# Attention with score products in bursts of three pairs on a three-entry PSUM ring

## The chip, the cores and the metric

One NeuronCore of one Trainium2 chip runs the kernel. The metric is device time in microseconds for one launch. In the profile PE is TensorE (PEld its weight loads), DVE VectorE, ACT ScalarE, POOL GpSimd, SP the engine that issues most DMAs.

## The reference

Cross-attention with 16 heads of 16 and a residual, then a mixture of 8 experts of which each token takes 2. The change touches the attention alone; what is computed is not changed.

```python
q, k, v = split(layernorm(x) @ wq.T + bq), split(ctx @ wk.T + bk), split(ctx @ wv.T + bv)
attn = softmax(einsum('bhqd,bhkd->bhqk', q, k) / 4)            # B=8, H=16, 512 x 512
x = x + (einsum('bhqk,bhkd->bhqd', attn, v) joined) @ wo.T + bo
x = x + sum over the top 2 of 8 experts: gate * (gelu(layernorm(x) @ W1 + b1) @ W2 + b2)
```

## The kernel before

The program runs in two stages: attention for all 8 batches (to about 550 us), and behind it the experts on sorted tokens. It is written engine by engine, each with its own program, and semaphores between them.

Attention is cut into 32 *units* u (batch i, group g of four heads), each unit into 8 *slots* p: one tile of 128 keys and two heads. For each slot of each unit two products of the same operands are made on TensorE, each a *pair* of matmuls (64 rows of the array for either head, 512 columns), into one entry of a ring of three PSUM tiles of 128 x 1024:

- `score(v, p)` (L1224, matmul L1233 of the page; MX in what follows): scores with queries on the partitions. DVE takes their row maximum (`reduce_max`, TENSOR_REDUCE at L860) into `negm`. It runs two units ahead: with slot (u, p) stands the MX of (u + 2, p) (`ahead`, L139).
- `score_t(u, p)` (matmul L1246; ST): the same scores transposed, with the maximum already subtracted through an extra row. ACT takes their exponential (L784) into `probs`.

The names of the lines: in the profile the page gives L1233 for MATMUL ring<-k_st,q_st and L1246 for MATMUL ring<-q_st,k_st; the weights of the first are q_st, of the second k_st.

`ring_order` (L147) writes down the order in which entries of the ring are claimed; `ORDER` and `PLACE` make it a numbering, entry = number mod 3. `slot(n)` (L1214) lets PE wait until the reader of claim n - 3 is done: `exp_done` if it was an ST, `max_free` if it was an MX.

Beside its two pairs a slot has *other products*, all on PE:

- `pv` (L1259): four products of `probs` and the values into `ps_pv`, in the slots p = 0 (the last of the unit before), 2, 4 and 6. When a unit is complete ACT copies them out (`take_o`, L774).
- `misc` by the tables PREP, NEXT, POST and so on (L35 to L48): projections Q, K, V (L1287, L1297), transposes XT, CT, XG of inputs (L1277), MT (L1268, the transpose of the maxima, at p = 0), the output projection OP (L1305), logits LG and ranks PX. All share one bank, `ps_x`; `claim` lets PE wait until the reader of the one before is done. ACT copies out Q, K, V, XT, CT, XG and MT; DVE takes OP, LG and PX.

ACT's program (its `body`) is, for each slot in order: exponential of ST, at p = 0 the copy of the pv sums, then the copies of the slot's misc products. DVE's is: the maximum of the slot's MX, then the slot's OP, LG or PX, then pieces of layer norms and routing. Both wait for PE at each step, in this fixed order.

PE's program `body` (L1331) takes each slot by itself: ST, MX, then pv and misc of that slot. In the middle batches each slot has some other product. In unit 0 the first slots have one ST and two MX, and in unit 26 on some slots have no other product.

Of the kernel before, what the change touches and what calls it, by code (L numbers as in the profile page):

```python
# [21 lines left out]
G = NG * B  # L22
# [7 lines left out]
NP = NT * HPG // 2  # L30
# [76 lines left out]
def units(i, g, p):  # L107

    u, out = NG * i + g, []
    if p == (2 if u == 0 else 0) and u + 1 < G:  # L110
        out.append(("MT", u + 1))
    last = i == B - 1
    for table, b in (((LAST_LATE if last else LATE), i - 2), ((LAST_POST if last else POST), i - 1),
                     ((FIRST if i == 0 else PREP), i + 1), (NEXT, i + 2)):
        if 0 <= b < B and (g, p) in table:
            out.append((table[g, p], b))
    return out
# [21 lines left out]
def ahead(u, p):  # L139

    if u == 0:
        rest = [(1, q) for q in range(NP // 2, NP)] + [(2, q) for q in range(NP)]
        return rest[2 * p:2 * p + 2] if p < NP // 2 else rest[p + NP // 2:p + NP // 2 + 1]
    return [(u + 2, p)] if u + 2 < G else []


def ring_order():  # L147
    order = [("MX", v, p) for v, p in EARLY]
    for u in range(G):
        for p in range(NP):  # L150
            order += [("ST", u, p)] + [("MX", v, q) for v, q in ahead(u, p)]
    return order


ORDER = ring_order()
PLACE = {op: n for n, op in enumerate(ORDER)}


def build(nc, x, ctx_kv, wqT, bq, wkT, bk, wvT, bv, woT, bo, wg, bg, w1, b1, w2, b2, out):
    with ExitStack() as stack:  # L160
# [1042 lines left out]
        def _(pe):  # L1203
# [10 lines left out]
            def slot(n):  # L1214

                if n >= RINGS:
                    kind, u, p = ORDER[n - RINGS]
                    pe.wait_ge(exp_done if kind == "ST" else max_free, NP * u + p + 1)
                else:
                    for k in (2 * n, 2 * n + 1):  # L1220
                        pe.wait_ge(done[last[k][0]], last[k][1])
                return ring[n % RINGS]

            def score(v, p):  # L1224

                b, g = divmod(v, NG)
                kt, jp = divmod(p, 2)
                if p == 0:
                    pe.wait_ge(stack_in[g], 16 * (5 * b + 4))
                ps = slot(PLACE["MX", v, p])  # L1230
                for h in range(2):
                    lo = HALF * h
                    mm = nc.tensor.matmul(ps[:, h, :], q_st[lo:lo + HALF, 2 * g + jp, kt * P:(kt + 1) * P],  # L1233
                                          k_st[lo:lo + HALF, 2 * g + jp, :], start=True, stop=True)
                mm.then_inc(max_full, 1)

            def score_t(u, p):

                b, g = divmod(u, NG)
                kt, jp = divmod(p, 2)  # L1240
                if p == 0:
                    pe.wait_ge(m_in[g], 16 * (b + 1))
                ps = slot(PLACE["ST", u, p])
                for h in range(2):
                    lo = HALF * h
                    mm = nc.tensor.matmul(ps[:, h, :], k_st[lo:lo + HALF, 2 * g + jp, kt * P:(kt + 1) * P],  # L1246
                                          q_st[lo:lo + HALF, 2 * g + jp, :], start=True, stop=True)
                mm.then_inc(st_full, 1)

            def pv(u, kt):  # L1250

                b, g = divmod(u, NG)
                pe.wait_ge(exp_done, NP * u + 2 * (kt + 1))
                if kt == 0:
                    if u > 0:
                        pe.wait_ge(o_out, u)
                    pe.wait_ge(v_in, NG * b + g + 1)
                for j in range(HPG):
                    mm = nc.tensor.matmul(ps_pv[2 * DH * j:2 * DH * (j + 1), :], v_aug[:, kt, HPG * g + j, :],  # L1259
                                          probs[:, kt, j, :], start=(kt == 0), stop=(kt == NT - 1))  # L1260
                mm.then_inc(pv_done, 1)
# [69 lines left out]
            def body(i):  # L1331
                for g in range(NG):
                    u = NG * i + g
                    for p in range(NP):
                        score_t(u, p)
                        for v, q in ahead(u, p):
                            score(v, q)
                        if p == 0 and u > 0:
                            pv(u - 1, NT - 1)
                        if p in (2, 4, 6):  # L1340
                            pv(u, p // 2 - 1)
                        for name, b in units(i, g, p):
                            misc(name, b)
# [17 lines left out]
            for i in range(B):  # L1361
                body(i)
# [90 lines left out]
```

## Time and profile before

| | us |
|---|---|
| three timed runs | 869.04 (median), 860.61, 870.62 |
| the profiled execution | 858.64 |
| its span, first to last instruction | 856.8 |
| PE busy | 766.0 |
| DVE busy | 630.3 |
| ACT busy | 452.4 |

The difference of 858.64 and 856.8 lies around the span. A line of the page names the source line, the engine, the operation, the tile written and those read. "[x <-ENGINE ...]" behind a row is idle time of that engine before the instruction and who ended it; on the load queue (PEld) idle time is mostly the time in which PE works off the matmuls before.

### The profile page before, as it was taken

What the parts mean: (1) busy time and instruction counts of PE and PEld (TensorE: products, weight loads), DVE (VectorE), ACT (ScalarE), POOL (GpSimd) and SP (SyncE); (2) the same over time, 40 slices, a digit from 0 to 9 for tenths busy, and PEclk for the clock granted to TensorE, in tenths of its full rate; (3) what the DMA queues carried; (4) which work ended last, traced back from release to release, by engine and by line L of the source; (5) the groups of instructions that cost most, each with busy time, mean ns of one, the idle gap of its engine ahead of it and who ended that gap; (6) DMA issues with size and microseconds to landing.
All of it is one profiled execution on the core that took longest, in us unless ns stands there. A gap on an engine that the chain in (4) does not pass through costs nothing. (4 is left out here: it accounts for less than half of the span.)

```text
span 856.8 us, 16256 instructions
## 1 busy us (share of the span) xinstructions
PE 766.0 (89%) x4697; PEld 460.4 (54%) x4697; DVE 630.3 (74%) x1113; ACT 452.4 (53%) x669; POOL 370.7 (43%) x342
## 2 busy tenths in 40 slices
PE   8599899999999999999999787331999999999995
PEld 4243344444444444444444332120899999999995
DVE  6786777797797797897787875365677777777774
ACT  3066775766766767766666555220444444444442
POOL 6406153266276176176244052304244444444444
PEclk9589999999999999999999988655999999999998
DMA  6857575676675676567367332244244444444441
GB/s 216 206 152 212 134 202 180 172 227 198 173 244 167 175 244 181 149 229 202 109 219 213 90 110 69 89 196 134 46 80 77 79 81 74 78 75 78 77 75 13
DMA packets 89083, 122.60 MB, mean 143 GB/s; under 512 B 15032, under 2 KB 51864, under 8 KB 88744
## 3 DMA queue, kind: packets, MB, share of 16 engines
q1 hardware_dynamic: 74632, 103.69, 42.2%
q0 software_dynamic: 13296, 17.09, 11.2%
q8 instruction: 43, 0.70, 0.4%
q10 hardware_dynamic: 1072, 0.79, 0.3%
q14 instruction: 40, 0.33, 0.1%
HBM read 64.44 MB, written 57.22 MB: 142 GB/s over the span
## 5 line engine op out<-in xcount | busy, mean ns | idle before, releaser
L860 DVE TENSOR_REDUCE negm<-ring 128x2 f32<-128x1024 f32 x256 | 310.3, 1222 | 76.9 <-PE ring L1233 74.7
L784 ACT ACTIVATE probs<-ring 128x1024 f32<-128x1024 f32 x256 | 260.7, 1024 | 98.0 <-PE ring L1246 97.6
L706 POOL DMA_INDIRECT out<-y_sb,xs x71 | 110.6, 1557 | 150.5 <-DMA out<-y_sb,xs 81.9
L1259 PE MATMUL ps_pv<-probs,v_aug 128*32 128x512 f32 x1024 | 138.6, 613 | 5.3 <-ACT probs L784 5.2
L1246 PE MATMUL ring<-q_st,k_st 64*128 64x512 f32 x512 | 128.0, 499 | 4.6 <-DVE negm L860 4.5
L1233 PE MATMUL ring<-k_st,q_st 64*128 64x512 f32 x512 | 110.4, 432 | 12.7 <-ACT probs L784 5.7
L1246 PEld LDWEIGHTS ring<-q_st,k_st 64*128 64x128 f32 x512 | 48.3, 186 | 105.8 <-issue 76.4
L612 POOL DMA_INDIRECT xs_dram<-xg,rows x64 | 65.4, 1021 | 81.0 <-DVEq L1023 51.1
L1404 PE MATMUL ring<-w_hi,hT_hi 128*128 x284 | 85.7, 302 | 0.1
L1404 PE MATMUL ring<-w_lo,hT_hi 128*128 x284 | 80.4, 283 | 0.0
L1404 PE MATMUL ring<-w_hi,hT_lo 128*128 x284 | 79.7, 281 | 0.0
L1171 DVE TENSOR_TENSOR h_pre<-ring,b_sb 128x512 f32<-128x512 f32 x71 | 49.1, 691 | 35.8 <-PE ring L1386 35.7
L654 POOL TENSOR_TENSOR v_aug<-v_flat,bv_sb 128x256 f32<-128x256 f32 x32 | 23.0, 736 | 99.5 <-PE ps_pv L1259 89.2
L1233 PEld LDWEIGHTS ring<-k_st,q_st 64*128 64x128 f32 x512 | 50.9, 195 | 27.5 <-DVE negm L860 8.8
L827 ACT CAST xsT_hi<-ps_pv 128x256 fp32r<-128x256 f32 x36 | 13.4, 373 | 88.6 <-PE ps_pv L1377 88.6
L1386 PE MATMUL ring<-w_hi,xsT_hi 128*128 x142 | 56.8, 400 | 1.7 <-DVE xsT_lo L1159 1.7
L1386 PE MATMUL ring<-w_lo,xsT_hi 128*128 x142 | 56.7, 399 | 0.0
L638 POOL CAST qk_hi<-qk 128x512 fp32r<-128x512 f32 x28 | 17.1, 610 | 91.4 <-ACT qk L749 60.9
L1386 PE MATMUL ring<-w_hi,xsT_lo 128*128 x142 | 56.5, 398 | 0.0
L1305 PE MATMUL ps_x<-wo_sb,numT 128*128 128x256 f32 x128 | 40.8, 447 | 15.5 <-DVE numT L896 13.9
L1404 PEld LDWEIGHTS ring<-w_lo,hT_hi 128*128 128x128 f32 x284 | 53.9, 190 | 0.0
L1404 PEld LDWEIGHTS ring<-w_hi,hT_hi 128*128 128x128 f32 x284 | 53.8, 189 | 0.2 <-issue 0.2
(167 smaller groups left out, 1240.5 us busy)
## 6 DMA issues: line engine op xcount, KB each, us to landing
k_st<-k_dram SPq DMA_DIRECT2D x64, 192.0 KB
q_st<-q_dram SPq DMA_DIRECT2D x64, 192.0 KB
xs<-xs_dram SPq DMA_DIRECT2D x71, 132.5 KB, 2.3
k_dram<-qk_hi SPq DMA_DIRECT2D x32, 256.0 KB
q_dram<-qk_hi SPq DMA_DIRECT2D x32, 256.0 KB, 2.9
o_dram<-oT SPq DMA_DIRECT2D x32, 256.0 KB, 3.9
x_all<-in_x SPq DMA_DIRECT2D x8, 512.0 KB, 4.9
k_dram<-qk_lo SPq DMA_DIRECT2D x16, 256.0 KB
```

The source lines that it names most:

```text
L612: pool.indirect_dma_start(out=xs_dram, out_offset=bass.IndirectOffsetOnAxis(ap=rows[:, k, t:t + 1], axis=0), in_=xg[:, t, :], in_offset=No ...
L654: nc.gpsimd.tensor_tensor(v_aug[:, :, HPG * g:HPG * (g + 1), 0:DH], v_flat[:, :, heads].rearrange("p t (h d) -> p t h d", d=DH), bv_sb[:, ...
L706: pool.indirect_dma_start(out=out, out_offset=bass.IndirectOffsetOnAxis(ap=xs[:, j % AHEAD, TOKEN:TOKEN + 1].bitcast(I32), axis=0), in_=y_ ...
L784: nc.scalar.activation(probs[:, kt, 2 * jp:2 * jp + 2, :], ring[PLACE["ST", u, p] % RINGS][:], ACT.Exp).then_inc(exp_done, 1)
L860: nc.vector.tensor_reduce(negm[:, v % 2, :, jp, kt], ring[PLACE["MX", v, p] % RINGS][:], AX.X, ALU.max, negate=True).then_inc(max_free, 1)
L1171: v.tensor_tensor(h_pre[:, j % 2, :], ps_h[j % 2], b1_sb[:, bass.ds(e, 1), :].rearrange("p o h -> p (o h)"), ALU.add).then_inc(f_h_out, 1)
L1233: mm = nc.tensor.matmul(ps[:, h, :], q_st[lo:lo + HALF, 2 * g + jp, kt * P:(kt + 1) * P], k_st[lo:lo + HALF, 2 * g + jp, :], start=True, s ...
L1246: mm = nc.tensor.matmul(ps[:, h, :], k_st[lo:lo + HALF, 2 * g + jp, kt * P:(kt + 1) * P], q_st[lo:lo + HALF, 2 * g + jp, :], start=True, s ...
L1259: mm = nc.tensor.matmul(ps_pv[2 * DH * j:2 * DH * (j + 1), :], v_aug[:, kt, HPG * g + j, :], probs[:, kt, j, :], start=(kt == 0), stop=(kt ...
L1305: mm = nc.tensor.matmul(ps[:, (t % 2) * D:(t % 2 + 1) * D], numT[:, c, t * P:(t + 1) * P], wo_sb[:, c, :], start=(c == 0), stop=(c == DC - 1))
L1386: mm = nc.tensor.matmul(ps_h[j % 2], x[:, j % 2, c, :], w[:, bass.ds(e, 1), c, :].rearrange("p o h -> p (o h)"), start=(n == 0), stop=(n = ...
L1404: mm = nc.tensor.matmul(ps_y[j % 2][:, 0:D], h[:, j % 2, c, :], w[:, bass.ds(e, 1), c, :].rearrange("p o d -> p (o d)"), start=(n == 0), s ...
```

## The change

The slots are taken in threes from (1, 0) on, 231 slots in 77 triples; `third(u, p)` gives a slot's place in its triple (0, 1, 2) or None outside. The first slot issues its ST and MX and the ST of the second slot, then its other products. The second issues its own MX and the ST and MX of the third, then its other products. The third issues its other products alone. `ring_order` is written to match. ACT's and DVE's programs are not touched.

```diff
+def third(u, p):
+    n = NP * (u - 1) + p
+    return n % 3 if 0 <= n < NP * (G - 3) // 3 * 3 else None
+
+def after(u, p):
+    return (u, p + 1) if p + 1 < NP else (u + 1, 0)
+
 def ring_order():
     order = [("MX", v, p) for v, p in EARLY]
     for u in range(G):
         for p in range(NP):
-            order += [("ST", u, p)] + [("MX", v, q) for v, q in ahead(u, p)]
+            place, own, maxima = third(u, p), [("ST", u, p)], [("MX", v, q) for v, q in ahead(u, p)]
+            if place == 0:
+                order += own + maxima + [("ST", *after(u, p))]
+            elif place == 1:
+                order += maxima + [("ST", *after(u, p))] + [("MX", v, q) for v, q in ahead(*after(u, p))]
+            elif place is None:
+                order += own + maxima
     return order
...
                     for p in range(NP):
-                        score_t(u, p)
-                        for v, q in ahead(u, p):
-                            score(v, q)
+                        place = third(u, p)
+                        if place in (0, None):
+                            score_t(u, p)
+                        if place != 2:
+                            for v, q in ahead(u, p):
+                                score(v, q)
+                        if place in (0, 1):
+                            score_t(*after(u, p))
+                        if place == 1:
+                            for v, q in ahead(*after(u, p)):
+                                score(v, q)
                         if p == 0 and u > 0:
                             pv(u - 1, NT - 1)
```

PE in unit 20, slots (20, 3) to (20, 5), before; L1246 is ST, L1233 MX, L1287 a projection, L1259 pv:

```order
L1246 MATMUL ring0<-q_st,k_st 128x512 x2
L1233 MATMUL ring1<-k_st,q_st 128x512 x2
L1287 MATMUL ps_x<-xnT,wq_sb 128x256 x2
L1246 MATMUL ring2<-q_st,k_st 128x512 x2
L1233 MATMUL ring0<-k_st,q_st 128x512 x2
L1259 MATMUL ps_pv<-probs,v_aug 32x512 x4
L1246 MATMUL ring1<-q_st,k_st 128x512 x2
L1233 MATMUL ring2<-k_st,q_st 128x512 x2
L1287 MATMUL ps_x<-xnT,wq_sb 128x256 x2
```

The same place after, from the triple's first slot (20, 4) to its end; lines have moved by 16, so L1262 is ST, L1249 MX, L1303 a projection, L1275 pv:

```order
L1262 MATMUL ring2<-q_st,k_st 128x512 x2
L1249 MATMUL ring0<-k_st,q_st 128x512 x2
L1262 MATMUL ring1<-q_st,k_st 128x512 x2
L1275 MATMUL ps_pv<-probs,v_aug 32x512 x4
L1249 MATMUL ring2<-k_st,q_st 128x512 x2
L1262 MATMUL ring0<-q_st,k_st 128x512 x2
L1249 MATMUL ring1<-k_st,q_st 128x512 x2
L1303 MATMUL ps_x<-xnT,wq_sb 128x256 x2
L1275 MATMUL ps_pv<-probs,v_aug 32x512 x4
```

A pair and one ring entry stood beside each other product before; now three pairs stand together, all three entries of the ring, then one slot's other products, three pairs, and two slots' others. Each entry keeps its reader and its place in the claims. The second burst's last pair writes ring1, which the first burst's last pair filled, with one product between the bursts.

ACT in the same unit, the same before and after up to the line numbers (L784 the exponential, L746 the copy of a Q projection; before):

```order
L784 ACTIVATE probs<-ring0 128x1024
L746 ACTIVATE qk32<-ps_x,bq_sb 128x256
L784 ACTIVATE probs<-ring2 128x1024
L784 ACTIVATE probs<-ring1 128x1024
L746 ACTIVATE qk32<-ps_x,bq_sb 128x256
L784 ACTIVATE probs<-ring0 128x1024
```

A slot's copy stands between that slot's exponential and the next slot's, as it did.

## Rows read from the trace of the kernel before

**Rows 1.** The page: busy us, share and instructions; PE's busy tenths in 40 slices.

```profile
PE 766.0 (89%) x4697; PEld 460.4 (54%) x4697; DVE 630.3 (74%) x1113; ACT 452.4 (53%) x669; POOL 370.7 (43%) x342
PE   8599899999999999999999787331999999999995
```

**Rows 2.** Stretches: length, busy PE, PEld, DVE, ACT, POOL; PE clock, DMA share, GB/s.

```profile
62.00:440.00 378.00, 372.20 (x2254) 167.34 (x2246) 301.18 (x477) 258.28 (x345) 180.13 (x181) 1.00 0.65 189
...
460.00:470.00 10.00, 8.86 (x59) 3.60 (x59) 7.90 (x7) 7.46 (x11) 3.16 (x5) 1.00 0.80 193
...
480.00:490.00 10.00, 7.92 (x61) 2.86 (x63) 9.37 (x27) 5.81 (x7) 0.00 (x0) 1.00 0.55 118
490.00:500.00 10.00, 7.12 (x27) 2.96 (x26) 5.12 (x7) 3.16 (x5) 6.87 (x7) 0.66 0.48 163
```

**Rows 3.** Groups of instructions, 62 to 440 us: busy us, mean ns, idle before.

```profile
L860 DVE TENSOR_REDUCE negm<-ring 128x2 f32<-128x1024 f32 x198 | 241.1, 1223 | 60.9 <-PE ring L1233 59.2
L784 ACT ACTIVATE probs<-ring 128x1024 f32<-128x1024 f32 x198 | 202.2, 1024 | 62.7 <-PE ring L1246 62.7
```

**Rows 4.** PE in order of time, unit 20: start us, duration us, what.

```profile
355.19 1.06 PE L1259 MATMUL ps_pv<-probs,v_aug 128*32 128x512 f32 x8
356.19 1.13 PE L1287 MATMUL ps_x<-kvT,wk_sb 128*128 128x256 f32 x4
357.25 0.50 PE L1246 MATMUL ring<-q_st,k_st 64*128 64x512 f32 x2
...
358.97 0.50 PE L1246 MATMUL ring<-q_st,k_st 64*128 64x512 f32 x2
...
359.63 1.06 PE L1259 MATMUL ps_pv<-probs,v_aug 128*32 128x512 f32 x8
360.63 0.49 PE L1246 MATMUL ring<-q_st,k_st 64*128 64x512 f32 x2
...
361.29 1.13 PE L1287 MATMUL ps_x<-xnT,wq_sb 128*128 128x256 f32 x4
362.35 0.50 PE L1246 MATMUL ring<-q_st,k_st 64*128 64x512 f32 x2
```

**Rows 5.** ACT in order of time, unit 20.

```profile
361.16 1.02 ACT L784 ACTIVATE probs<-ring 128x1024 f32<-128x1024 f32 x1 [0.63 <-PE ring L1246]
362.46 0.47 ACT L746 ACTIVATE qk<-ps_x,bq_sb 128x256 f32<-128x256 f32 x1 [0.27 <-PE ps_x L1287]
362.89 1.03 ACT L784 ACTIVATE probs<-ring 128x1024 f32<-128x1024 f32 x1
```

**Rows 6.** PE in order of time, unit 0: one ST and two MX.

```profile
50.61 0.50 PE L1246 MATMUL ring<-q_st,k_st 64*128 64x512 f32 x2
...
51.50 1.13 PE L1287 MATMUL ps_x<-kvT,wk_sb 128*128 128x256 f32 x4
```

**Rows 7.** Engines in order of time, end of unit 26: a slot without other products.

```profile
458.76 0.19 PEld L1246 LDWEIGHTS ring<-q_st,k_st 64*128 64x128 f32 x2 [0.84 <-issue]
...
459.31 1.94 ACT L784 ACTIVATE probs<-ring 128x1024 f32<-128x1024 f32 x2 [0.58 <-PE ring L1246]
...
459.54 1.23 DVE L860 TENSOR_REDUCE negm<-ring 128x2 f32<-128x1024 f32 x1 [0.43 <-PE ring L1233]
460.44 0.21 PEld L1233 LDWEIGHTS ring<-k_st,q_st 64*128 64x128 f32 x2 [1.01 <-issue]
...
460.91 1.07 PE L1259 MATMUL ps_pv<-probs,v_aug 128*32 128x512 f32 x8
```

**Rows 8.** Engines in order of time, behind an MT transpose.

```profile
306.71 0.50 PE L1246 MATMUL ring<-q_st,k_st 64*128 64x512 f32 x2
...
307.12 0.25 ACT L755 CAST mT<-ps_x 16x128 fp32r<-16x128 f32 x1
...
307.42 0.73 PEld L1287 LDWEIGHTS ps_x<-kvT,wk_sb 128*128 128x128 f32 x4 [0.41 <-ACT mT L755]
```

**Rows 9.** Waits of the load queue, 62 to 440 us: sum, times, longest.

```profile
PEld ring L1246 <- DVE negm L860: 13.5, 18, 1.3
```

## The prediction, written before the changed kernel was run

> **What bounds the kernel now.** I read the page's shares first, then the busy times by stretch, then the groups of the attention stretch, and last the order of time on PE and ACT. PE is busy for 766.0 of 856.8 us [rows 1]. From 62 to 440 us, where attention runs in its steady form, it is busy for 372.20 of 378.00 us at a granted clock of 1.00, while DVE has 301.18 and ACT 258.28 [rows 2]. In that stretch stand 198 exponentials and 198 maxima [rows 3], so one slot takes 378.00 / 198 = 1.91 us. PE sets the pace, and whatever makes it wait there is added to the end. ACT and DVE have room on average, but a ring of three entries feeds them, so it matters *when* PE asks for an entry back.
>
> The slot's parts come from the starts on PE [rows 4]. A burst of two score pairs takes 359.63 - 358.97 = 0.66 us until the next product starts; the four pv products take 360.63 - 359.63 = 1.00; a projection of 256 columns takes 362.35 - 361.29 = 1.06. A burst of three pairs, which unit 0 has, takes 51.50 - 50.61 = 0.89 [rows 6]. So a pair costs 0.23 and the entry into a burst 0.20.
>
> On ACT [rows 4, 5]: an exponential starts 0.53 after its burst starts when ACT is free (360.63 to 361.16) and takes 1.02. The copy of a projection starts 0.11 after PE has left the projection (362.35 to 362.46), and the exponential behind it starts 0.43 later (362.89). Two exponentials that are both ready start 1.94 - 1.02 = 0.92 apart [rows 7].
>
> **The change, part by part.** Call the slots of a triple 0, 1, 2, their pairs ST0, MX0, ST1, MX1, ST2, MX2, and their other products o0, o1, o2. 231 slots make 77 triples. The ring's entries are claimed in the same order as before, nothing is added or removed, and the rows of ACT, DVE, POOL and SP stand in the same order with the same ring numbers. Only PE's order moves: before, burst(2), o0, burst(2), o1, burst(2), o2; after, burst(3), o0, burst(3), o1, o2. No DMA is issued differently.
>
> *What it takes away.* Three bursts of 0.66 become two of 0.89: 1.98 - 1.78 = 0.20 us a triple, 77 x 0.20 = 15.4 us. o1 and o2 standing together I price at nothing: in most triples one is pv and the other a product of full width, and each kept its own time in the rows whatever stood ahead of it.
>
> One rule bears on this term. The trace shows that pv keeps its 1.00 us whether a projection or a burst stands behind it (355.19 to 356.19, 359.63 to 360.63), and the projection behind pv its 1.06 [rows 4]: each block carries its own entry, so one block fewer is a gain. The Trainium skill, "TensorEngine Tiling (Array Packing)", section Key Properties, says that a change of the tiling mode drains TensorE; taken by itself this would let the step from o1 to o2 cost as much as the one that it replaces, the gain would be 0 and the sum below 15.4 us higher. I go by the row. The same page, section PSUM Bottleneck, speaks against the change: tiling makes TensorE faster but not the emptying of PSUM. What that does here is the next term, worked out from rows alone.
>
> *The stall in the second burst.* MX2 writes the entry that ST1 filled, three places earlier. Before, o0 was over when ST1 came, and MX1, o1 and ST2 followed until MX2 asked for the entry. Now ST1 comes ahead of o0, and MX2 asks behind o0 and two pairs. And ACT takes its work in the old order: exponential of ST0, copy of o0, exponential of ST1. The copy can't start before PE has done o0. So where o0 holds something that ACT copies (projections, transposes, the MT transpose with the pv copy), counted from the end of o0: 0.11 until the copy, 0.43 until the exponential of ST1, 1.02 for it, 0.11 until PE reloads, 0.47 for a pair that starts alone. The last two are read where the unchanged kernel has four pairs in a row: exponential from 459.31 to 460.33, reload at 460.44, next product at 460.91 [rows 7]. Sum 2.14, against 0.89 without the wait: 1.25 us. Behind this PE wait stand MX2, o1, o2 and with them every engine. By the tables of units 42 of the 77 triples have such an o0: 52.5 us. Copies of 512 columns, or the pv copy and then MT's, would be longer: MT's copy starts 307.12 - 306.71 = 0.41 after PE's next product has started, and the 0.25 of its own follow [rows 8]. I put that at up to 0.15 and leave it in the range.
>
> Where o0 has nothing for ACT, the exponentials run one behind the other: 0.53 + 0.92 + 1.02 + 0.11 + 0.47 = 3.05 us from the start of the first burst to the end of the second, against 0.89 + 1.00 + 0.89 = 2.78: 0.27 us, in 31 triples 8.4 us. In four triples o0 is empty: 3.05 - 1.78 = 1.27 each, 5.1 us. So even the kindest triple loses more than the 0.20 that it saves.
>
> *The stall in the next first burst.* MX0 of the next triple takes the entry of ST2, and the exponential of ST2 stands on ACT behind the copy of o1. From the end of o1: 0.11 + 0.43 + 1.02 + 0.11 = 1.67 until MX0 may load, then 0.47 + 0.23, together 2.37, against 1.00 (o2 = pv) + 0.89: 0.48. 26 triples have this, some with a longer o2 that hides it; at 0.4 each, 10 us. In 13 triples o1 has an ACT copy and o2 is a product alone that needs the same bank ps_x: it waits for the copy, 0.11 + 0.47 or so, 0.6 each, 8 us. Before, a burst stood between the two, so such a wait was short (306.71 + 0.66 = 307.37 against 307.42, 0.05 us) [rows 8]. The dozen triples where DVE or nothing stands in o1 or o2 get 6 us by the same working.
>
> *DVE.* MX0's maximum must be done for ST2. It starts 0.78 after the burst [rows 7] and takes 1.22 [rows 3]: with the 0.11 to the reload 2.1 after the burst's start, against 0.89 + 1.00 + 0.1 = 2.0 when ST2 comes. That fits by a hair when DVE has no side work left, and in 42 triples the exponential is later anyway. I price it at nothing; if the side work of each triple held PE for another 0.5 us, it would cost 38 us; that is the upper end. Some waits that PE has now would vanish beside the longer ones: the loads' wait for DVE sums to 13.5 us in 18 places, most of which is the usual gap [rows 9]; I take -4.
>
> Sum: -15.4 + 52.5 + 8.4 + 5.1 + 10 + 8 + 6 - 4 = +70.6 us. The profiled execution took 858.64 us, so 929.2. The three timed runs have a median 10.4 above it; I add half of that: 934 us. What lies behind attention (from 600 us) doesn't change and shifts.
>
> **The rivals.**
> - *Faster.* Only the bursts count: 858.6 - 15.4 = 843 us. This is one mechanism: ACT would have ST1's entry free when MX2 comes. It decides at o0's end + 0.23; ACT needs o0's end + 1.67. For it speaks only that ACT idles between exponentials (0.63 before one) [rows 5]; against it, that this idle time is the wait for PE which the copy's place in the order causes. Chance 0.03.
> - *No change.* The copies somehow don't hold the exponentials back, and all triples pay only 0.27: 77 x 0.07 = +5 us, 864 to 870. Chance 0.05.
> - *Half of it.* Stalls overlap: a wait of PE gives ACT and DVE time that the next wait doesn't need again, and the second kind is hidden. About +35 us, 894 to 903. Chance 0.10.
> - *DVE joins.* The 38 us above on top: 972 us. Its side work comes in clumps; against it speaks DVE's 80% share, which gets smaller per slot. Chance 0.12.
> - *The clock falls.* With waits in each triple PE would be busy for about 5.7 of 6.6 us, 87%. At 460 to 490 us it was busy 8.86 and 7.92 of 10 and the clock stayed at 1.00; at 7.12 of 10, in one long pause, it was 0.66 [rows 2]. If it averaged 0.9, the 440 us of PE work would gain about 45: 980 us. Chance 0.06.
>
> **How the numbers follow.** The forecast has 0.64. It alone spans 910 to 955: 0.15 on 42 triples upward, the second kind of stall (24 us) downward. To leave out no more than two in ten, the range goes to 900 below, into the half case, and to 968 above, nearly to the DVE case. Slower by over 2% holds the forecast, the half case, DVE and the clock: 0.92. Within 2% (about what timing this kernel can tell from no change) 0.05, faster 0.03.
>
> **What would show it.** In the profile of the changed kernel the waits of PE or its loads for "ACT probs" in the score lines should grow from a few us to 60 and more, many of them 1.0 to 1.3 us long; ACT's idle time before its exponentials should not shrink; a burst of three without a wait should take 0.89; exponentials and maxima should keep 1.02 and 1.22; PE's busy share between 70 and 500 us should fall to some 87% at a clock near 1.00; the part behind attention should keep its length. I am wrong if MX2 is seen to start 0.23 after ST2 in triples whose o0 is a projection, or if the waits name DVE's negm in most places.

## The result and the profile after

The changed kernel takes 925.06 us (median of 4 runs, 923.93 to 927.69) against 867.36 us of the kernel before: 1.0727 times as long, 95% interval 1.067 to 1.0784. The forecast was 934 (900 to 968). The profiled execution took 924.77 us, 66.1 more than that of before. Against the median of about 862 us that the kernel before has beside the experiments, the loss is 63 us; against the 867.36 us it is 58.

First the page of the changed kernel: busy us and shares, and PE's busy tenths. The rows answer to [rows 1].

```profile
PE 787.8 (85%) x4697; PEld 471.1 (51%) x4697; DVE 626.9 (68%) x1113; ACT 447.2 (48%) x669; POOL 370.9 (40%) x342
PE   8598899888989898888988987743299999999995
```

The work is the same, the span is longer, and the digits 8 in the attention part are new; the last third, the experts, is all 9 as before. The stretch of attention, busy us of PE, PEld, DVE, ACT, POOL, then clock, against [rows 2]:

```profile
62.00:440.00 378.00, 334.77 (x1940) 151.63 (x1936) 258.36 (x410) 218.94 (x297) 160.73 (x160) 0.97 0.57 166
```

PE falls from 372.20 to 334.77 busy us in the same 378: 89%. The groups of the two readers from 62 to 500 us, against [rows 3]:

```profile
L876 DVE TENSOR_REDUCE negm<-ring 128x2 f32<-128x1024 f32 x198 | 240.3, 1222 | 103.0 <-PE ring L1249 101.9
L800 ACT ACTIVATE probs<-ring 128x1024 f32<-128x1024 f32 x198 | 197.4, 1022 | 29.0 <-PE ring L1262 28.4
```

The same 198 slots now need 438 us instead of 378: 2.21 us a slot instead of 1.91, 0.9 us a triple. Neither reader got slower (1222 and 1022 ns). ACT even waits less directly before its exponentials (29.0 instead of 62.7 us). Its waiting has moved to the copies: before those of K and Q it now idles 37.5 and 32.1 us in this stretch, where before it was 15.3 and 11.4 us. The waits of PE and of its load queue, 62 to 500 us (sum, times, longest):

```profile
PE ring L1249 <- ACT probs L800: 35.7, 49, 1.3
...
PEld ring L1249 <- ACT probs L800: 70.9, 93, 1.5
...
PEld ring L1262 <- DVE negm L876: 20.0, 33, 1.4
```

L1249 is MX; the name behind it is the exponential whose entry it wants. On the load queue this was 5.0 us from 62 to 440 us and 7.9 us from 62 to 500 before. One triple shows the mechanism, PE first, then ACT:

```profile
400.06 1.78 PE L1303 MATMUL ps_x<-kvT,wk_sb 128*128 128x256 f32 x4
401.77 0.50 PE L1249 MATMUL ring<-k_st,q_st 64*128 64x512 f32 x2
402.11 0.40 PE L1262 MATMUL ring<-q_st,k_st 64*128 64x512 f32 x2
403.32 0.50 PE L1249 MATMUL ring<-k_st,q_st 64*128 64x512 f32 x2 [0.82 <-ACT probs L800]
403.76 1.07 PE L1275 MATMUL ps_pv<-probs,v_aug 128*32 128x512 f32 x8
404.75 1.13 PE L1303 MATMUL ps_x<-kvT,wk_sb 128*128 128x256 f32 x4
406.45 1.13 PE L1303 MATMUL ps_x<-xnT,wq_sb 128*128 128x256 f32 x4 [0.56 <-ACT qk L765]
407.51 0.50 PE L1262 MATMUL ring<-q_st,k_st 64*128 64x512 f32 x2
...
408.41 1.07 PE L1275 MATMUL ps_pv<-probs,v_aug 128*32 128x512 f32 x8
409.41 0.50 PE L1249 MATMUL ring<-k_st,q_st 64*128 64x512 f32 x2
...
410.48 1.13 PE L1303 MATMUL ps_x<-xnT,wq_sb 128*128 128x256 f32 x4
```

```profile
401.88 0.47 ACT L765 ACTIVATE qk<-ps_x,bk_sb 128x256 f32<-128x256 f32 x1 [1.53 <-PE ps_x L1303]
402.25 1.02 ACT L800 ACTIVATE probs<-ring 128x1024 f32<-128x1024 f32 x1
```

The second burst starts at 401.77, when o0 (K0a, half of a K projection, from 400.06) is over. ACT copies K0a at 401.88, starts the exponential of ST1 at 402.25 and ends it at 403.27; MX2 starts at 403.32. ST1 had been ready all the while: ACT had idled 1.53 us ahead of the copy, because the copy stands before it in the program. (TensorE ran at half clock until 401.4, so K0a took 1.71 us instead of 1.06, and this idle time is longer than usual; the wait behind it is not.) The burst takes 403.76 - 401.77 = 1.99 us instead of 0.89. At 406.45 stands the third kind of stall, o2 waiting for the copy that empties ps_x. The next triple has pv alone as o0: its first burst takes 0.90, its second 410.48 - 409.41 = 1.07.

The same can be read for all 77 triples, each from the start of its ST0 on PE to the start of the next triple, and compared with the same slots before. Of the 42 triples whose o0 has a copy for ACT, 35 ran at the full clock in both executions; they are 1.22 us longer on average. Of the 31 whose o0 has none, 28 did; they are 0.05 us longer. Of the 4 with an empty o0, 3 did; they are 0.34 us longer. Over all 77 that is 54 us, 51 of them in the 42 triples where the prediction put the stall. The whole stretch from the start of slot (1, 0) to that of slot (29, 7), after and before:

```profile
61.50:569.50 508.00, 450.07 (x2614) 203.29 (x2613) 350.56 (x563) 292.13 (x392) 205.49 (x208) 0.96 0.56 161
```

```profile
60.70:506.60 445.90, 432.57 (x2614) 193.16 (x2613) 353.81 (x563) 297.59 (x392) 204.87 (x208) 0.99 0.63 184
```

The work is the same (2614 matmuls) and the stretch is 62 us longer. What the triples at full clock leave, 8 us, goes with the clock: in this stretch it stood at its lower level (1.2 GHz) for 37.5 us after and 10.2 us before. The 4 us that are left of the 66 lie outside this stretch.

### The profile page after: what moved, and what is told of

It is laid out like the page before. It is cut to its first block and busy times, and to the rows that moved or that the text cites. A ratio compares the mean times of both kernels' runs of the same rounds, so it can differ in the third digit from the quotient of the medians.

```text
span 922.9 us, 16256 instructions
## 1 busy us (share of the span) xinstructions
PE 787.8 (85%) x4697; PEld 471.1 (51%) x4697; DVE 626.9 (68%) x1113; ACT 447.2 (48%) x669; POOL 370.9 (40%) x342
## 5 line engine op out<-in xcount | busy, mean ns | idle before, releaser
L800 ACT ACTIVATE probs<-ring 128x1024 f32<-128x1024 f32 x256 | 255.1, 1022 | 62.3 <-PE ring L1262 61.3
L1249 PE MATMUL ring<-k_st,q_st 64*128 64x512 f32 x512 | 125.8, 492 | 46.4 <-ACT probs L800 38.9
L1275 PE MATMUL ps_pv<-probs,v_aug 128*32 128x512 f32 x1024 | 146.2, 645 | 4.5 <-ACT probs L800 4.3
L1262 PE MATMUL ring<-q_st,k_st 64*128 64x512 f32 x512 | 118.4, 461 | 8.1 <-DVE negm L876 7.6
L1249 PEld LDWEIGHTS ring<-k_st,q_st 64*128 64x128 f32 x512 | 51.2, 197 | 114.8 <-ACT probs L800 79.7
L1262 PEld LDWEIGHTS ring<-q_st,k_st 64*128 64x128 f32 x512 | 50.1, 193 | 60.7 <-DVE negm L876 29.7
```

Source lines behind the costliest of these rows:

```text
L800: nc.scalar.activation(probs[:, kt, 2 * jp:2 * jp + 2, :], ring[PLACE["ST", u, p] % RINGS][:], ACT.Exp).then_inc(exp_done, 1)
```

## The experiments

Times of before are the medians of its runs beside each experiment, 861.5 to 862.1 us. Differences are taken from the medians.

**The copies out of the way of ST1's exponential (act_first).** The exponential moved into a function; PE and DVE untouched.

```diff
 for p in range(NP):           # ACT's body
-    exponential(u, p)
+    place = third(u, p)
+    if place in (0, None):
+        exponential(u, p)
+    if place == 0:
+        exponential(*after(u, p))
+    if place == 2:
+        exponential(u, p)
```

> The changed kernel with one thing moved on ACT: in each triple the exponential of ST1 stands ahead of the copies of o0 (the exponential of ST2 stays behind the copies of o1). PE's order is that of the change. Theory (the copy of o0 holds back ST1's exponential, and MX2 waits for it): in 42 triples the wait shrinks from 1.25 to 0.27 us, so 41 us less: 925 - 41 = 884 us, and PE's waits for ACT probs before MX fall from some 36 us to under 15. Rival (the three-entry ring is too short for bursts of three whatever ACT's order, or DVE is the one that is late): under 10 us less, above 915 us.

Measured: 880.77 us (1.0227 of before, 1.0151 to 1.0303). 44 us less than the changed kernel, where the theory said 41. Its waits on the load queue from 62 to 500 us:

```profile
PEld ring L1259 <- ACT probs L798: 34.9, 73, 1.4
...
PEld ring L1272 <- DVE negm L886: 30.4, 53, 1.8
```

L1259 is MX, L1272 ST. The wait for ACT is halved, that of PE itself is 5.9 us in 15 places up to 560 us, and the wait for DVE has grown by 10 us: it was hidden behind ACT's. Nothing but the order on ACT differs. At full clock the 42 triples with a copy are now 0.28 us longer than before instead of 1.22, which is 40 us less over all 42; a second burst with a copy in o0 takes 1.11 us on average instead of 2.05. So the copy's place in ACT's order made some two thirds of the loss of 63 us directly. The clock gave back some 8 us more: 10.2 us at the lower level between the slots (1, 0) and (29, 7), as in the kernel before. The 44 us measured are close to the 41 foretold partly because other small terms went the other way.

**Both copies out of the way (act_both).** As above, with `if place in (0, 1): exponential(*after(u, p))` and no line for place 2.

> As act_first, and the exponential of ST2 also stands ahead of the copies of o1. Theory: the second stall (0.4 us in 26 triples, 10 us) goes too: 874 us. If the second stall was hidden behind DVE or the ps_x bank anyway: the same as act_first within 3 us.

Measured: 878.24 us (1.0179, 1.0101 to 1.0257), 2.5 us less than act_first, which runs that spread over 5 us don't tell from nothing. But the traces tell more than the medians. Behind a triple whose o1 has a copy and whose o2 is pv alone, the first burst takes 1.43 us in act_first and 1.15 here (14 and 13 triples at full clock); over all 77 triples, at full clock, act_both is 8 to 9 us shorter. The profiled execution of act_both had 20.5 us at the lower clock between the slots (1, 0) and (29, 7), act_first's 10.2, and a longer end of attention. Over the whole program the four executions of act_both had a mean clock of 0.921 to 0.927, those of act_first 0.927 to 0.934, which can hide most of the gain. So the second stall was about as large as foretold.

**The maxima together on DVE as well (act_dve).**

```diff
-for v, q in ahead(u, p):      # DVE's body
-    reduce_max(v, q)
+place = third(u, p)
+if place != 2:
+    for v, q in ahead(u, p):
+        reduce_max(v, q)
+if place == 1:
+    for v, q in ahead(*after(u, p)):
+        reduce_max(v, q)
```

> As act_both, and on DVE the maxima of MX1 and MX2 both stand ahead of DVE's reading of o1 and the side work of that slot. Theory: DVE was no bound, 0 to 4 us less than act_both, about 872 us; OP reads come later, which costs ps_x waits. Rival (DVE's clumps hold PE): 15 us or more less than act_both.

Measured: 878.88 us (1.0212, 1.0137 to 1.0288), the same as act_both within what runs that spread over 7 to 8 us can tell. The order on DVE costs nothing that can be measured here.

**Half of the triples (half_triples).** `third` ends at n < 117 instead of 231: 39 of 77 triples.

> The change for the first 39 of the 77 triples only, the old order behind them. Theory (a price per triple, at a place): about half of the 58 to 66 us, so 893 to 900 us. Rival (a cost paid once, as by the clock or by a disturbed late stage): near 867 or near 925.

Measured: 891.28 us (1.034, 1.0268 to 1.0412): +29 us over before for 39 triples, 0.75 each, and 34 for the 38 others, 0.89 each. The cost goes with the number of triples; it isn't paid once.

**The time of DVE (halfmax, halfmax_before, halfmax_act).** The reductions read `[:, :, 0:S // 2]`. In all three the maximum leaves out half of the keys.

> The changed kernel with the maxima taken over half of the columns (the other half of each row is left out of the maximum), so that each of DVE's 256 reductions takes some 0.7 instead of 1.22 us. Theory (ACT is the late one): 2 to 8 us less, 917 to 923 us, PE's waits for ACT probs unchanged. Rival (DVE holds the ring): 25 us less or more, under 900 us.

> The kernel before with the maxima taken over half of the columns (the other half is left out of the maximum). A control for halfmax (21 us less on the changed kernel): if DVE costs the kernel before next to nothing, 855 to 860 us, and some 15 us of the change's loss are DVE's; if the late stage beyond 480 us gains by it in any kernel, some 850 us and less is DVE's.

> act_both with the maxima over half of the columns (the other half left out). With the copies out of ACT's way DVE should be the larger part of what is left: 878 - 15 to 20 = 858 to 863 us. If what is left is the two exponentials (0.27 us in 73 triples, 20 us) alone: 870 us or more.

Measured: the changed kernel 903.78 us (two executions, 21 less), the kernel before 848.15 us (two executions, 846.39 and 849.91, 13 less), act_both 857.51 us (median of seven; an eighth took 866.74; 21 less). The first number was a miss for the theory: it said 2 to 8. The control takes most of it back, since the kernel before gains 13 us by the same edit; what DVE adds to the loss is the difference, 21 - 13 = 8 us at most. Part of it is the clock again, 17.1 us at the lower level in the changed kernel with half maxima against 37.5 us: at full clock the 77 triples lose 51 us between the two kernels with half maxima and 54 between the two without, so some 4 us are DVE's own. For act_both the third expectation gives nearly the right time, but by luck in part: it took DVE for the larger part of what is left, while 13 of the 21 us are what the kernel before gains by the same edit. In the changed kernel with half maxima the waits (load queue, 62 to 500 us) read:

```profile
PEld ring L1249 <- ACT probs L800: 75.8, 96, 1.5
...
PEld ring L1262 <- DVE negm L876: 6.6, 9, 0.8
```

DVE's part is all but gone and ACT's has stayed (70.9 to 75.8): with DVE nearly twice as fast on the maxima (0.69 instead of 1.22 us), the loss is still 903.78 - 848.15 = 56 us between the two kernels with half maxima. That excludes DVE as the main cause.

**The other products divided 2 and 1 (split21).** o0 and o1 behind the first burst, o2 alone behind the second.

```diff
-if place in (0, None):
-    score_t(u, p)
-if place != 2:
-    for v, q in ahead(u, p):
-        score(v, q)
-if place in (0, 1):
-    score_t(*after(u, p))
-if place == 1:
-    for v, q in ahead(*after(u, p)):
-        score(v, q)
+if place in (0, None):
+    score_t(u, p)
+    for v, q in ahead(u, p):
+        score(v, q)
+if place == 0:
+    score_t(*after(u, p))
+if place == 2:
+    for v, q in ahead(*prev(u, p)):
+        score(v, q)
+    score_t(u, p)
+    for v, q in ahead(u, p):
+        score(v, q)
```

> The changed kernel with o0 and o1 together behind the first burst and o2 alone behind the second (MX1, ST2 and MX2 come after o1). Theory: the wait moves to where two readers of one engine must finish beside one product: between the second burst and the next first one stand the two maxima MX1 and MX2 (0.54 + 2 x 1.22 + 0.11 us against 2.2 when ST1 comes), about 0.75 us a triple, 58 us, and 0.2 in 42 triples at the second burst: 905 to 920 us, with DVE negm named in the waits instead of ACT probs. Rival (any split with a burst of three costs what the copies on ACT cost): the waits still name ACT probs.

Measured: 922.76 us (1.07, 1.0622 to 1.0779), a little above the range that was given. The profiled execution had 51.2 us at the lower clock between the slots (1, 0) and (29, 7), which makes some 20 us of its loss; at full clock its triples lose 41 us together, 0.53 each, less than the 0.75 of the theory and than the 54 us of the changed kernel. Its waits on the load queue, 62 to 500 us (L1266 ST, L1253 MX):

```profile
PEld ring L1266 <- DVE negm L880: 62.7, 81, 2.5
...
PEld ring L1253 <- ACT probs L804: 9.9, 26, 1.7
```

As foretold the name has changed: with the same number of bursts another engine holds the ring. Which reader PE waits for depends on how the other products are divided between the bursts. That the times of the two kernels are nearly equal is the clock's doing in part.

**Triples only where o0 is long, ACT's order old and new (select_old, select).** `third` looks slots up in a table that is built from the starting slots; `select` adds the order of act_both.

```diff
+def choose(starts):
+    chosen, n = {}, NP
+    while n + 2 < NP * (G - 2):
+        u, p = divmod(n, NP)
+        if (u % NG, p) in starts:
+            for place in range(3):
+                chosen[divmod(n + place, NP)] = place
+            n += 3
+        else:
+            n += 1
+    return chosen
...
+CHOSEN = choose({(0, 2), (0, 7), (1, 6), (2, 3), (2, 5), (3, 4), (3, 6)})
```

> Triples only where o0 is long (pv with a projection or transpose, or a product of 1.9 us): slots (0,2), (0,7), (1,6), (2,3), (2,5), (3,4), (3,6) of the four units of a batch, which gives 35 triples; the other slots in the old order; ACT's order untouched. Theory (MX2 waits for the copy of o0 and the exponential behind it, and both start only when o0 is over, so a long o0 is no cover): about 30 triples pay 1.25 us and 35 save 0.20: 862 + 37 - 7 = 892 us. Rival (the time between the two bursts is what counts, a long o0 gives it): 850 to 860 us.

> The same 35 triples, and ACT's order as in act_both. Theory: the two exponentials (2.5 us from the first burst's start) now run beside an o0 of 1.9 us or more and are over when MX2 comes, so only the saving of 0.20 is left: 862 - 7 = 855 us, 0.8% faster than before. If the entry cost of a burst is not saved: 862 us.

Measured: select_old 895.86 us (1.0407, 1.0339 to 1.0475), select 865.71 us (1.0059, 1.0021 to 1.0096, 12 runs). The first is close to what was foretold: 35 triples with a long o0 lose 34 us, although nearly 2 us stand between the bursts of most. Triple by triple at full clock, those at (0,2), (2,3) and (3,4) mostly lose 0.9 to 1.0 us each, those at (0,7) 1.84, and six of the seven at (1,6), where DVE takes the o0 and ACT has no copy, gain 0.20. (No triple starts at (2,5) or (3,6), since those at (2,3) and (3,4) cover them.) One that starts at (0,7), on PE:

```profile
324.88 1.98 PE L1317 MATMUL ps_x<-xnT,wq_sb 128*128 128x512 f32 x4
326.79 0.49 PE L1263 MATMUL ring<-k_st,q_st 64*128 64x512 f32 x2
327.13 0.40 PE L1276 MATMUL ring<-q_st,k_st 64*128 64x512 f32 x2
328.56 0.50 PE L1263 MATMUL ring<-k_st,q_st 64*128 64x512 f32 x2 [1.03 <-ACT probs L814]
```

The wait behind a 1.91 us product is longer than that behind K0a, because the copy is longer too (0.69 us instead of 0.47). The second is 11 us above what was expected. Its trace shows where, on PE in order of time:

```profile
306.68 0.49 PE L1284 MATMUL ring<-q_st,k_st 64*128 64x512 f32 x2 [1.06 <-DVE negm L898]
...
311.82 1.13 PE L1325 MATMUL ps_x<-kvT,wk_sb 128*128 128x256 f32 x4 [0.64 <-ACT mT L785]
...
320.09 0.49 PE L1284 MATMUL ring<-q_st,k_st 64*128 64x512 f32 x2
...
320.99 1.06 PE L1297 MATMUL ps_pv<-probs,v_aug 128*32 128x512 f32 x8
```

The first two belong to the triple that starts at (0, 7). Its first burst ends with ST1, which wants the entry of the maximum before, and DVE is behind with the layer norm and routing of slots (0, 4) to (0, 6); then (1, 1) stands right behind MT and waits for ps_x. The triple at (1, 6) runs its first burst in 0.90 with no wait. Between 105 and 440 us the list of PE's waits has no others than these two kinds, the first four times and the second six. With ACT's order moved the triples at (0,7) still lose 1.78 us each, after 1.84 in select_old: the wait for ACT is gone and one for DVE has come in its place. Most of the 28 other triples are 0.18 to 0.21 us shorter than before.

**Without those triples (select_clean).** The starts are {(0, 2), (1, 6), (2, 3), (3, 4)}: 28 triples.

> select without the seven triples that start at slot (0,7), which are the ones whose first burst waits 1.06 us for DVE (side work of slots (0,4) to (0,6)) and behind which the projection of (1,1) waits 0.64 us for MT's copy; 28 triples are left. Theory (a burst of three is worth 0.20 us where nothing waits): 862 - 28 x 0.20 = 856 us, that is 0.4 to 1% faster than before and about 9 us faster than select. If the entry cost isn't saved: 862 us, the same as before.

Measured: 855.82 us (0.9947 of before, 0.9913 to 0.998; 12 runs against 23). As expected to the microsecond. Its trace agrees: the 27 triples at full clock are 0.22 us shorter than the same slots before on average, 20 of them by 0.18 to 0.20, and from slot (1, 0) to (29, 7) it takes 440.2 us against 445.9, with the same 10.2 us at the lower clock. It is the only version that beats both kernels: 69 us less than the changed one, and 0.5% less than the one before, with an interval that stays below 1; it is a small gain, within the 2% that single timings can tell.

## Why the prediction was right

The direction, the mechanism and its place were right; the time was 9 us high, and it would have been 17 high but for a slower clock that the forecast had not priced in. Point by point:

- *What bounds the kernel.* PE set the pace and any wait of PE was added to the end. Shown: PE's work is unchanged, and the slot grew from 1.91 to 2.21 us.
- *The burst.* A burst of three without a wait takes 0.90 us (407.51 to 408.41) against 0.89 forecast. That it saves 0.20 a triple is borne out by select_clean: 28 triples, 5.6 us expected, 5.7 measured, with an uncertainty of about 3 in the medians, and 20 of 27 triples at full clock show 0.18 to 0.20. The rule that a step from o1 to o2 would cost as much as the one it replaces would have made this zero; the projection behind pv keeps its duration of 1.13 (404.75), and where o1 has a copy and pv begins o2, the two together take 0.03 us less than they took apart (24 triples).
- *The stall in the second burst.* Forecast 2.14 us from the end of o0, measured 1.99 in the triple shown: the exponential came 0.37 after the copy instead of 0.43, and PE went on 0.05 after it instead of 0.11. Over 34 such bursts at full clock the mean is 2.05, from 1.83 to 2.19: 1.16 more than 0.89 instead of 1.25, which in 42 triples gives 49 us instead of 52.5. Where o0 has nothing for ACT, the mean of 28 is 1.01: 0.12 instead of 0.27, 4 us instead of 8. The prediction has MX2 asking for its entry 0.23 after o0's end; in the triple without a copy it comes at 410.05, 0.64 after. The sum doesn't use this figure.
- *The stall in the next first burst.* About right. Behind an o1 with a copy and pv alone as o2 the first burst takes 1.44 us in the changed kernel (13 triples at full clock), 0.55 more than 0.89, where 0.48 was forecast; with a longer o2 it takes 1.02. That act_both gave back only 2.5 us between medians goes with its lower clock.
- *The bank ps_x.* 0.56 us behind K0b against 0.6 forecast; in ten triples of this kind at full clock o1 and o2 together take 0.74 more than apart, 10 us in 13 triples where 8 were forecast; no experiment took it alone.
- *DVE.* Priced at nothing; by the half-maximum kernels it is 4 us at full clock and at most 8. It became the second of the waits as soon as ACT's were gone (20.0 to 30.4 us on the load queue).
- *The clock* I gave as a rival, as an average of 0.9. It came to a small part, 0.96 on average between the slots (1, 0) and (29, 7) against 0.99 before: the 27 us more at the lower level cost some 8 us, by what the triples at full clock leave. This is worked out from one profiled execution of each kernel.
- *The sum.* The forecast of 70.6 us stands against 54 in the triples at full clock, DVE's 4 included. Of the 16 too many, 4 are in the copies, 5 where o0 has nothing for ACT, and 3 in the triples with an empty o0 (0.34 us measured where 1.27 less 0.20 was forecast); the remainder lies in the smaller terms and wasn't taken apart. I also added 5 us for the gap between the profiled execution and the median; the changed kernel has no such gap (924.77 against 925.06). Against these 21 us stand the clock's 8 and the 4 outside the triples, neither of which the sum had. That 9 are left is luck in part.
- *The signs that I named.* MX's waits for ACT of over 1.0 us: yes, up to 1.5 us long, and 70.9 us in all on the load queue from 62 to 500 us. PE's share falling to 87%: 89%, at a clock of 0.97 and not near 1.00. ACT's idle before its exponentials "should not shrink": wrong, it fell from 62.7 to 29.0 us, and the idle time went to the copies.

## What to carry to other kernels

When one engine's program is reordered to make longer bursts, write beside it the programs of the engines that empty the buffer: an engine that takes its work in order can be held by a step that waits for a product issued later, and then the buffer isn't free although its reader idles. The time between two uses of a buffer is no measure of slack if the reader's turn comes only at the end of that time. Where a burst fills the whole ring, choose the places for it from the trace, one wait at a time; here 28 triples were worth having, and most of them only with ACT's order moved along with PE's. And where two medians differ by less than the clock can make, compare the same slots at the same clock in the two traces.

## What was not expected of the hardware

The granted clock fell for short times inside busy attention, without long pauses around. These are the stretches right before and in such a time in the changed kernel, then the same in the kernel before (columns as above).

```profile
316.00:322.90 6.90, 5.63 (x46) 3.27 (x44) 4.03 (x7) 3.18 (x4) 0.00 (x0) 1.00 0.42 132
322.90:329.80 6.90, 6.50 (x27) 2.26 (x19) 4.46 (x12) 3.22 (x7) 0.73 (x1) 0.51 0.44 136
```

```profile
407.00:413.90 6.90, 6.89 (x52) 3.93 (x52) 5.39 (x8) 4.58 (x6) 0.00 (x0) 1.00 0.15 53
414.00:417.40 3.40, 3.40 (x13) 1.76 (x9) 1.98 (x4) 1.95 (x5) 0.73 (x1) 0.50 0.18 67
```

In the changed kernel PE was busy for 5.63 of the 6.90 us before the clock fell; in the kernel before it was busy for all but 0.01. The busy share inside the slow time itself says little, since products take longer there: a projection of 256 columns takes 1.83 us (415.79 to 417.62 in the kernel before) instead of 1.06. I had read from the rows only that the clock holds at a busy share of 79 to 89%, and falls in a long pause; how often it falls in between I could not have said, and no run here settles what sets it off. It does move the time of a run: 6.8 to 51.2 us between the slots (1, 0) and (29, 7) at the lower level in the profiled executions of these kernels, some 8 us of time between the kernel before and the changed one.
